# Expert tiles of a mixture-of-experts layer: rows gathered by token lists and added to DRAM, instead of scattered by slot and combined by choice

## What is computed

```python
x = x + attention(layernorm(x), ctx_1024, ctx_1024, Wq, bq, Wk, bk, Wv, bv, Wo, bo)
xf = layernorm(x).reshape(2048, 256)
logits = xf @ gate_w.T
topk_logits, topk_idx = top_k(logits, 2)
topk_w = softmax(topk_logits)
comb = zeros((2048, 8)).at[arange(2048)[:, None], topk_idx].add(topk_w)
for e in range(8):
    y = silu(xf @ wg[e].T) * (xf @ wu[e].T) @ w_down[e].T
    out = out + comb[:, e:e + 1] * y
shared = silu(xf @ sg_gate.T) * (xf @ sg_up.T) @ sg_down.T
x = x + shared + out
```

## Time and profile before

| | |
|---|---|
| median of three runs | 576.96 us |
| lowest and highest | 576.51, 578.29 us |
| span of the profiled execution, first to last instruction | 575.3 us |
| its own time | no other than its span is recorded |
| TensorE busy | 482.2 us (84% of the span) |
| VectorE, ScalarE, GpSimd busy | 287.6, 204.3, 161.4 us |
| mean granted TensorE clock | 0.933 |
| HBM read, written | 27.05, 16.59 MB |

### The profile page before, as it was taken

One profiled execution on the slowest core, in us unless ns is written; L12 is line 12 of the kernel. 1 busy time (PEld: TensorE's weight loads), 2 busy tenths in 40 slices (PEclk: granted clock), 3 DMA queues, 4 the chain that ended last, 5 costly groups with the idle time before them and its releaser, 6 DMA issues.

```text
span 575.3 us, 9801 instructions
## 1 busy us (share of the span) xinstructions
PE 482.2 (84%) x2849; PEld 312.9 (54%) x2850; DVE 287.6 (50%) x590; ACT 204.3 (36%) x415; POOL 161.4 (28%) x186
## 2 busy tenths in 40 slices
PE   4536896999978997998879999279999999999890
PEld 2314442474424642473353555268888888888650
DVE  6746373647555572646544666114343433434357
ACT  1213464544536163544663444013232323232110
POOL 7004342312324043311211287601222222221200
PEclk9957799999979998998999999779999999999995
DMA  8759229191837539290207422212222222221168
GB/s 267 171 54 112 65 54 144 39 174 38 122 72 111 137 65 129 53 159 2 83 3 291 173 86 93 98 40 64 57 66 62 65 64 64 64 64 55 37 191 255
DMA packets 48193, 56.66 MB, mean 98 GB/s; under 512 B 10640, under 2 KB 43472, under 8 KB 47536
## 3 DMA queue, kind: packets, MB, share of 16 engines
q1 hardware_dynamic: 44768, 47.10, 38.0%
q0 software_dynamic: 3408, 9.34, 4.5%
HBM read 27.05 MB, written 16.59 MB: 76 GB/s over the span
## 4 chain that ended last, share of the span: by engine, by line
PE 53%; DMA 12%; DVE 9%; issue 7%; ACT 7%; POOL 6%; SPq 5%; ACTq 0%; POOLq 0%; DVEq 0%
PE set_b L889 9%; DMA attention<-attention 7%; POOL x_by_slot L555 6%; PE set_a L873 6%; PE set_a L592 5%; PE set_a L875 5%; PE set_a L874 5%; PE set_b L622 5%; SPq L357 5%; ACT attention L987 4%; PE set_a L643 3%; PE set_b L612 3%; DVE attention L1190 3%; PE set_a L798 2%; PE set_b L881 2%
## 5 line engine op out<-in xcount | busy, mean ns | idle before, releaser
L1190 DVE TENSOR_REDUCE attention<-set_a 128x2 f32<-128x1024 f32 (+2 forms) x96 | 96.7, 1042 | 57.5 <-PE set_a L594 55.6
L987 ACT ACTIVATE attention<-set_b 128x512 f32<-128x512 f32 (+1 forms) x176 | 87.5, 565 | 69.4 <-PE set_b L612 68.7
L592 PE MATMUL set_a<-attention 96*128 96x512 bf16 (+3 forms) x256 | 67.8, 330 | 32.7 <-DMA attention<-attention 26.0
L564 POOL DMA_INDIRECT y_by_choice<-moe,e_dst x39 | 37.2, 955 | 140.4 <-DVE moe L1372 131.8
L521 POOL TENSOR_SCALAR_AFFINE_SELECT attention<-attention 128x512 f32<-128x512 f32 x64 | 39.8, 634 | 116.3 <-ACT attention L987 116.2
L592 PEld LDWEIGHTS set_a<-attention 96*128 96x128 bf16 x256 | 26.7, 104 | 80.1 <-issue 46.2
L612 PE MATMUL set_b<-attention 99*128 99x512 bf16 (+3 forms) x256 | 60.8, 312 | 11.0 <-ACT attention L987 6.0
L1358 DVE TENSOR_TENSOR moe<-set_a,moe 128x384 f32<-128x384 f32 x39 | 21.7, 557 | 92.0 <-ACT moe L1075 92.0
L889 PE MATMUL set_b<-w_down,moe 128*128 x234 | 60.3, 388 | 1.1 <-DVE moe L1372 1.1
L1075 ACT ACTIVATE moe<-set_a 128x384 f32<-128x384 f32 x39 | 19.1, 490 | 116.7 <-PE set_a L875 116.7
L873 PE MATMUL set_a<-wup_hi,e_xT_hi 128*128 x156 | 57.1, 366 | 1.6 <-DVE e_xT_lo L1353 1.2
(11 more groups left out here) (152 smaller groups left out, 691.3 us busy)
## 6 DMA issues: line engine op xcount, KB each, us to landing
attention<-attention SPq DMA_DIRECT2D x96, 128.0 KB, 5.7
wup<-in_wupT SPq DMA_DIRECT2D x2, 3072.0 KB, 14.1
x_by_slot<-attention SPq DMA_DIRECT2D x13, 387.0 KB, 7.4
moe<-x_by_slot SPq DMA_DIRECT2D x39, 128.0 KB, 2.0
moe<-y_by_choice SPq DMA_DIRECT2D x16, 256.0 KB, 3.8
attention<-in_ctxT SPq DMA_DIRECT2D x7, 512.0 KB, 5.9
w_down<-in_wdnT SPq DMA_DIRECT2D x3, 1024.0 KB, 8.6
x_res<-in_x SPq DMA_DIRECT2D x4, 512.0 KB, 7.2
```

The lines of the kernel that those rows point to most:

```text
L592: mm(dst, qstack[0:ROWS, g // 2, h, k * P:w], kstack[0:ROWS, g // 2, h, 0:w], start=True, stop=False)
L987: nc.scalar.activation(pT[k][:, h:h + heads, :], bank(par)[:, 0:heads * (S - k * P)], ACT.Exp).then_inc(b_free, 1)
L1190: v.tensor_reduce(dst, src, AX.X, ALU.max, negate=True).then_inc(a_free, 1)
```

## The change

GpSimd no longer scatters before the tiles and SP no longer loads them. Four DMAs write the normed rows in token order to `normed_rows` in DRAM. VectorE turns each slot number into a tile number (`slot_hi`) and a place in the tile (`slot_lo`), and builds 0/1 tables: `at_slot`, 32 tables of 128 columns, and `at_tile`, which holds token numbers and the weights in three bf16 parts where the tile number fits. 32 TensorE products of the two (195 columns, `hot_full`) give `token_of` and `weight_of`: token and weight for each place of each tile. GpSimd gathers each tile's rows with an indirect DMA by `token_of` (`rows_in_tile`), and adds each weighted result to `sum_rows` in DRAM with an accumulating indirect DMA (`add_rows`), which waits until the one before has landed. `sum_rows` is filled beforehand with residual plus shared expert, so all four batches of the shared expert run before the tiles, with two instead of three pairs of PSUM banks, and the pieces of the up weights are split after batches 2 and 3. At the end one DMA copies `sum_rows` to `out`. The `zero_rows`, `y_by_choice` and `combine` are gone. The core of the diff:

```diff
 @sync
-                    zero_rows(4 * b + 1)
...
-                    zero_rows(4 * b + 2)
-                    zero_rows(4 * b + 3)
...
+            for b in range(B - 1):
+                sp.wait_ge(xs_ready, B + b + 1)
+                sp.dma_start(rows_of(xn_d, b), xn2[:, b * QT:(b + 1) * QT, :]).then_inc(xn_stored, DMA)
             sp.wait_ge(a_free, A_ALL)
             for c in range(C):
                 sp.dma_start(wup[:, c, :], wupT[c * P:(c + 1) * P]).then_inc(ld_up, DMA)
...
+            for b in range(B):
+                sp.wait_ge(s_yfree, b + 2)
+                sp.dma_start(rows_of(acc, b), xs_all[:, b * QT:(b + 1) * QT, :]).then_inc(acc_stored, DMA)
+
+            sp.wait_ge(added, DMA * NT)
+            sp.dma_start(out.rearrange("b (k p) d -> (b k) (p d)", p=P),
+                         acc[0:N].rearrange("(t p) d -> t (p d)", p=P)).then_inc(stored, DMA)
 @gpsimd
+            def rows_in_tile(t):
+                g.indirect_dma_start(e_x[:, t % 2, :], None, xn_d,
+                                     bass.IndirectOffsetOnAxis(token_of[:, t:t + 1], 0)).then_inc(e_in[t % 2], DMA)
+
+            def add_rows(t):
+                pool.wait_ge(added, DMA * t)
                 pool_turn(e_yr, t + 2)
+                g.indirect_dma_start(acc, bass.IndirectOffsetOnAxis(token_of[:, t:t + 1], 0),
+                                     e_y[:, t % 2, :], None, compute_op=ALU.add).then_inc(added, DMA)
+
+            for t in range(3):
+                if t > 1:
+                    pool_turn(e_xt, t - 1)
+                rows_in_tile(t)
+            pool.wait_ge(acc_stored, DMA * B)
+            for t in range(NT):
+                if t + 3 < NT:
+                    pool_turn(e_xt, t + 2)
+                    rows_in_tile(t + 3)
+                add_rows(t)
 @tensor
             def shared_up(b, lo=0, hi=M):
                 for m in range(lo, hi):
-                    for w, dst in zip((wsg, wsu), gu[m]):
+                    n = b * M + m
+                    if n > 1:
+                        pe.wait_ge(s_h, n - 1)
+                    for w, dst in zip((wsg, wsu), gu[n % 2]):
...
             shared_up(0, 1)
-            pe.wait_ge(slots_ready, TOP_K)
+            pe.wait_ge(rank_read, 2)
             shared_down(0)
-
-            for b in range(1, N_SHARED_1):
+            shared_up(1)
+            pe.wait_ge(hot_built, 1)
+            for j in range(NJ):
+                last = mm(Bk[:, 0, 0:NCOL * NT], at_slot[:, j, :],
+                          at_tile[:, j, :, :].rearrange("p c t -> p (c t)"), start=j == 0, stop=j == NJ - 1)
+            last.then_inc(hot_full, 1)
+            shared_down(1)
+            for b in range(2, B):
                 shared_up(b)
                 shared_down(b)
 @scalar
-                if b == 0:
+                if b == 1:
                     act.wait_ge(ld_up, DMA * C)
-                    act.wait_ge(wts_ready, 1)
+                    act.wait_ge(lists_ready, 1)
 @vector
+            link(v.tensor_tensor(in_tile, per_row(slot_hi),
+                                 io_tile.rearrange("p (o t) -> p o t", o=1).to_broadcast([P, NJ, NT]),
+                                 ALU.is_equal))
...
+            for i in range(3):
+                v.tensor_tensor(at_tile[:, :, 2 + i, :], in_tile, per_row(wpart[:, i]), ALU.mult)
+            shared_y(0)
...
+            hot_slots(range(0, T))
+            shared_h(1, 0)
+            hot_slots(range(T, NJ)).then_inc(hot_built, 1)
...
                 dve.wait_ge(e_yf, t + 1)
-                v.tensor_copy(e_y[:, a, :], Bk[:, 2, 0:D]).then_inc(e_yr, 1)
+                v.tensor_scalar(e_y[:, a, :], Bk[:, 2, 0:D], weight_of[:, bass.ds(t, 1)], None,
+                                ALU.mult).then_inc(e_yr, 1)
```

More of the change, by code:

```diff
@@ L401, in batch @@
                                  ).then_inc(ld_moe, DMA)
-            sp.wait_ge(pad_rows, 1)
-            zero_rows(0)
+            sp.wait_ge(fills, 3)
+            for rows in (xn_d, acc):
+                sp.dma_start(rows[N:N + P, :], zeros).then_inc(pad_rows, DMA)
             max_rows(1, B_GRP0 + MAX_AT)
@@ L1097, in _ @@
             hidden_t(NT - 1, 0)
-            for b in range(N_SHARED_1, B):
-                shared_silu(b)
         @block.vector
@@ L1340, in _, with hot_slots @@
             link(v.reciprocal(wts[:, 0, :], sm))
-            v.tensor_tensor(wts[:, 1, :], ex, wts[:, 0, :], ALU.mult).then_inc(wts_ready, 1)
-            for b in range(N_SHARED_1):
+            link(v.tensor_tensor(wts[:, 1, :], ex, wts[:, 0, :], ALU.mult))
+            link(v.tensor_copy(wpart[:, 0], wts))
+            link(v.tensor_tensor(wrem, wts, wpart[:, 0], ALU.subtract))
+            link(v.tensor_copy(wpart[:, 1], wrem))
+            link(v.tensor_tensor(wpart[:, 2], wrem, wpart[:, 1], ALU.subtract))
+            for i in range(3):
+                v.tensor_tensor(at_tile[:, :, 2 + i, :], in_tile, per_row(wpart[:, i]), ALU.mult)
+            shared_y(0)
+            def hot_slots(js):
+                for j in js:
+                    k, t = divmod(j, T)
+                    last = v.tensor_scalar(at_slot[:, j, :], io_slot, slot_lo[:, k, t:t + 1], None, ALU.is_equal)
+                return last
+            hot_slots(range(0, T))
+            shared_h(1, 0)
+            hot_slots(range(T, NJ)).then_inc(hot_built, 1)
+            shared_h(1, 1)
+            shared_h(1, 2)
+            dve.wait_ge(hot_full, 1)
+            lists = Bk[:, 0, 0:NCOL * NT].rearrange("p (c t) -> p t c", c=NCOL)
+            link(v.tensor_reduce(tok, lists[:, :, 0:2], AX.X, ALU.add))
+            v.tensor_reduce(weight_of[:], lists[:, :, 2:NCOL], AX.X, ALU.add)
+            v.tensor_scalar(token_of[:], tok, io_np, None, ALU.add).then_inc(lists_ready, 1)
+            shared_y(1)
+            for b in range(2, B):
                 for m in range(M):
@@ L1392, in _ @@
                 pair_of_tiles(i, True)
[L1393 to L1420 removed]
+            result(NT - 3, 0)
+            result(NT - 2, 1)
+            result(NT - 1, 0)
 def kernel(x, ctx_1024, L0_xattn_Wq, L0_xattn_bq, L0_xattn_Wk, L0_xattn_bk, L0_xattn_Wv, L0_xattn_bv,
```

224 lines of the change are left out of this document (82 added, 142 removed).

## The result

The changed kernel takes **743.47 us** (median of four runs, 740.88 to 748.38) where the kernel before takes 576.74 us beside it: a ratio of 1.289, 95% interval 1.283 to 1.294. The profiled execution took 741.85 us, its span is 740.1 us.

The account below looks back on a forecast made before the run. TensorE was taken to bound the loop before, the closed gather-and-add chain after. Terms 121 + 22.4 - 2.5 - 14.8 + 1 = +127 on the 575.3 us span gave 702.4, plus 1.7 for the median: 704 us, range 662 to 757.

Parts of the forecast that it names:

- The mechanism: Expert loop: tile t+4's gather stands behind tile t's add on GpSimd, closing a chain that paces passes; +121 us.
- (c): Rival, expert loop: GpSimd's chain does not hold the gather, 4.14 us per pass, front as forecast; 583 us, chance 0.02.
- (d): Rival: gather not held, front bound by TensorE alone, faster final copy, shorter attention; 571 us, chance 0.04.
- The pass: Expert loop: one closed chain from transposes to transposes, 7.1 us at full clock for 4.14 before, bounds 6.4 and 7.5.
- GpSimd's own time: Expert loop: GpSimd's time on the add, a step of the pass, put at 0.95 us.
- gather's landing: Expert loop: the gather from issue to landing, 2.4 us as the indirect write, lower bound 2.0 as a plain load.
- The clock: Expert loop: pauses put three passes in ten at half clock, adding 0.5 us, so the pass is 7.6 us.
- Rival (a): Expert loop: TensorE's clock falls in every pass, 8.8 us each; 746 us, chance 0.13.
- Rival (b): Expert loop: the accumulation lands late and sets the pace above 6.2 us; at 8 us, 750 us; chance 0.06.
- Attention: Attention stage: the 13 zero-row DMAs go, operands start earlier in three batches; -2.5 us, bounds -4.5 and 0.
- Ahead of the first tile: Routing and shared expert: fourth batch, lists, stalls and VectorE's last low parts delay the first tile; +22.4 us, bounds +15 and +30.
- The end: After the last write: one DRAM copy, 10.5 us, replaces 25.3 us, -14.8; three accumulations in sequence, +1; bounds -18 and +1.

Follow-up runs that it names:

- e1: Changed kernel with each gather issued one place earlier on GpSimd, the rows of tile t+4 before the add of tile t: 596.4 us.
- e2: Changed kernel with plain scattering DMAs in place of the adding ones, so the sums are left out: 711.5 us.
- e3: Changed kernel with 18 idle matmuls in each pass, put where TensorE waits for gathered rows: 720.8 us.
- e8: Kernel before, with the 13 zeroing DMAs moved from the attention to behind the up-weight loads, and a separate source of zeros: 588.0 us.
- e6: e1 with tiles added by turns to two DRAM tensors, leaving out every second tile's results: 575.6 us.
- e5: Changed kernel with gathers one place earlier and the up weights split one shared batch earlier: 591.8 us.
- e12: e5 with an unused array of 128 B per partition laid ahead of the attention's buffers: 583.1 us.

## Why the prediction came out as it did

**The mechanism** of the loop was right, and the time, 704, was 5% low. The gather behind the add on GpSimd's queue closes a loop over the steps below; its removal (e1) takes 147 of the 167 us. The rivals (c) and (d), in which the gather would not be held, are near to what e1's order gives, and not this one's: e1 is 13 us above (c)'s 583, for a reason (c) did not have, the chain of adds.

**The pass, 7.1 forecast, 8.05 measured** at full clock, is the term that was mis-sized. By step:

| step | forecast | measured |
|---|---|---|
| transposes and down products to the copy | 1.80 | 2.05 |
| copy, now a multiplication | 0.42 | 0.49 |
| to GpSimd's start | 0.80 | 0.80 |
| GpSimd's own time | 0.95 | 1.59 |
| to the gather | 0.6 | 0.30 |
| gather's landing | 2.4 | 2.76 |
| to TensorE | 0.14 | 0.05 |

The step that failed is "GpSimd's own time 0.95": I took it from the plain scatter, unbounded. e2 shows that the addition alone is the difference, 0.6 us. The gather's landing was bounded by 2.0 and 2.4 (and 0.2 more), both below what it was. The step to the gather was 0.30, the lower bound: here the semaphore step between two indirect DMAs, its wait long met, cost nothing over the 0.30 of back-to-back ones. The upper bound of 7.5 was therefore too low by 0.55 us, or 19 us of the total.

**The clock**: the mean pass is 0.65 us above the full-clock one, 0.5 forecast. e3 confirms the size by removing it: 22.7 us between the medians. How it comes about was forecast wrongly, and that the size is near is in part luck: not three passes in ten wholly at 1.2 GHz and the rest at full clock, but 25 of 35 slow for a part, 8 of them from their start. Nor does a slow pass leave nearly no pause: behind the pass of 9.44 us, at 0.68, TensorE still waited 2.48 us for rows. Rival (a), 746, is nearest to the result by its number. It was right that the clock falls in most passes, but it had 1.7 us for it in each, where the mean is 0.65, and a loop of 7.1; the two errors cancel. The rule of the Trainium skill ("TensorE: Matmul & The Clock Gate", section "HAM oscillation — how this bites in real kernels"), by which a loop that waits for a DMA in every pass is throttled in every pass, held in most passes here and not in all: the granted clock was below 1.00 in 26 of 35 and 1.00 in nine, and 0.85 over the loop.

**Rival (b)**, the add's landing as the pace from 6.2 us on: it landed in 3.8 us. It did pace e1, at 4.59.

**Attention**: -4.0 for -2.5, within the bounds, but that the zeroing is the cause is not shown. The changed kernel and e8 leave it out of the attention and gain 4.0 and 4.75 us, but both also moved the buffers (landings 5.5 and 5.6 us for 5.7), and no run left out the zeroing with the buffers in their place. Moreover, kernels with the same attention code and placement (e1 to e6) ended it between 298.6 and 301.5, so that a difference of 1.5 us there means little, and what makes that spread is open.

**Ahead of the first tile**: +20.3 for +22.4. The three waits for shared_h are there (1.67, 1.18 and 1.72 us for 2 each), the table rows took 1.45 us each as worked out from the shapes, and the last four low parts with the add ahead of them 8 us. The 32 small tables took 5.4 us for 6.4.

**The end**: -11.1 for -13.8. From the last write's issue it is 12.75 us for 27.7 before, -14.9 as forecast (the copy 9.1 us for 10.5, the landing longer by 1.2; at 8.7 us from issue to landing the copy is also faster than the 11.7 that the prediction gives for reading and writing counted together); but the last results take 3.8 us more to get out, for 1 forecast, since three adds wait for each other at 4.56 us.

In sum: between the spans the forecast was 37.7 us short (127.1 for 164.8); the passes alone were 38.6 short (33 for the loop, 5 for the clock), and the other three terms cancel to within 1 us. One sum of the prediction does not come out of its parts: passes of 6.7 to 8.2 us with all the other bounds give 659 to 750, not 668 to 730. The range given, 662 to 757, holds the result either way.

## What to carry to other kernels

When a transfer is put behind another on an in-order queue, follow it around: if the second one's result is needed for the first one's input some passes later, the whole round trip becomes the pace, and one place earlier in the order can be worth more than all other edits (here 147 us of 743). Price a DMA operation that the trace doesn't show on both sides of its nearest relative, the issuing engine's own time too. And look at where buffers lie before believing a gain in a stage that no edit touched.

## What the runs showed of the hardware

- An indirect DMA of 128 rows of 1 KB in the expert loop occupied GpSimd for 0.95 to 0.99 us when it scattered or gathered, 1.55 to 1.59 us when it added; it landed 2.4 (scatter), 2.8 (gather) and 3.8 us (add) after its issue.
- Adds to one DRAM tensor that wait for each other followed at 4.56 to 4.61 us in the mean (e1, e5, e12, and the end of the changed kernel); to two by turns, at the loop's 4.15.
- With TensorE waiting for a DMA in each pass of the changed kernel's loop, the granted clock fell below 1.00 in 26 of 35 passes and was 0.85 in the mean; 18 idle matmuls in each wait held it at 1.00 and saved 23 us.
- Copies within SBUF landed in 5.0 to 5.1 us with the buffers at a multiple of 512 B and in 5.5 to 5.7 at three other places; moved from one of these to the multiple (e5 to e12), the attention ended 7.3 us earlier.
- A VectorE product of two SBUF inputs took 3.23 us for 1.45 beside a GpSimd product, and a small operation 2.23 for 0.17.
